# Graph attention with residual and layer norm on one core: normalising of finished rows moved from ScalarE to GpSimd, all but the last half chunk

## The reference

```python
mask = adj + eye > 0
Wh = (x @ W.T).reshape(n, 4, 32)
e = score_l[:, :, None] + score_r.T[None, :, :]      # per node and head
e = where(e >= 0, e, 0.2 * e)
e = where(mask[:, None, :], e, -inf)
alpha = softmax(e, axis=2)
out = elu(einsum('nhm,mhd->nhd', alpha, Wh).reshape(n, 128))
z = x + out
y = (z - mean(z)) / sqrt(var(z) + 1e-5)              # over the 128 features
```

## Time and profile before

| | us |
|---|---|
| median of 3 runs | 1782.24 |
| lowest and highest of the 3 | 1779.88, 1790.67 |
| the profiled execution, its own time | 1779.54 |
| its span, from the first to the last instruction | 1777.8 |

### The profile page before, as it was taken

One profiled execution on the slowest core, in us unless ns is written; L12 is line 12 of the kernel. 1 busy time (PEld: TensorE's weight loads), 2 busy tenths in 40 slices (PEclk: granted clock), 3 DMA queues, 4 the chain that ended last, 5 costly groups with the idle time before them and its releaser, 6 DMA issues. The chain is left out here.

```text
span 1777.8 us, 80971 instructions
## 1 busy us (share of the span) xinstructions
PE 1647.8 (93%) x37067; PEld 1626.5 (91%) x37067; DVE 1685.2 (95%) x1905; ACT 1667.8 (94%) x1246; POOL 26.2 (1%) x36
## 2 busy tenths in 40 slices
PE   6788898999999999999999999999999999999995
PEld 6788798899999999999999999999999998999995
DVE  6999999998979989999999999999899999999997
ACT  4999999989899999999999999999999999999992
POOL 0000000000001000000000100000000100000000
PEclk9899999999999999999999999999999999999998
DMA  8996888999998876675766676676667131121111
GB/s 278 344 346 206 277 293 266 341 313 328 310 307 293 257 246 198 205 243 182 244 202 223 207 242 215 209 235 208 224 189 236 35 82 58 37 58 37 35 37 37
DMA packets 241476, 368.10 MB, mean 207 GB/s; under 512 B 12912, under 2 KB 103408, under 8 KB 239600
## 3 DMA queue, kind: packets, MB, share of 16 engines
q1 hardware_dynamic: 241136, 362.92, 62.9%
HBM read 345.57 MB, written 17.30 MB: 204 GB/s over the span
## 5 line engine op out<-in xcount | busy, mean ns | idle before, releaser
L505 ACT ACTIVATE bmask<-lrow,rtab 128x2048 fp8e4<-128x2048 f32 (+1 forms) x975 | 1547.9, 1666 | 49.8 <-PE psum L414 47.5
L414 PE MATMUL psum<-vring,cmask 128*128 128x99 bf16 x14336 | 716.4, 208 | 30.5 <-DVE cmask L730 26.5
L414 PE MATMUL psum<-vring,bmask 128*128 128x99 bf16 x14336 | 722.0, 208 | 19.2 <-issue 15.6
L414 PEld LDWEIGHTS psum<-vring,cmask 128*128 128x128 fp8e4 x14336 | 662.0, 98 | 42.5 <-DVE cmask L730 35.8
L414 PEld LDWEIGHTS psum<-vring,bmask 128*128 128x128 fp8e4 x14336 | 667.4, 97 | 21.3 <-issue 17.5
L730 DVE SCALAR_TENSOR_TENSOR cmask<-acache,bmask 128x1024 int32<-128x1024 int32 x512 | 623.5, 1218 | 19.8 <-PE psum L414 19.5
L725 DVE SCALAR_TENSOR_TENSOR bmask<-acache,bmask 128x1024 int32<-128x1024 int32 x512 | 624.1, 1219 | 8.4 <-ACT bmask L505 4.6
L706 DVE TENSOR_SCALAR bmask<-lrow,rtab 128x2048 fp8e4<-128x2048 f32 (+1 forms) x305 | 316.8, 1052 | 0.0
L383 PE MATMUL trp<-pack,abuf 128*128 128x64 bf16 x4096 | 143.9, 194 | 32.3 <-ACT acache L474 23.5
L383 PEld LDWEIGHTS trp<-pack,abuf 128*128 128x128 bf16 x4096 | 132.6, 99 | 35.2 <-issue 35.0
L414 PE MATMUL psum<-vt,bmask 128*128 128x99 bf16 x2048 | 107.1, 211 | 12.2 <-issue 9.7
(11 more groups left out here) (64 smaller groups left out, 264.1 us busy)
## 6 DMA issues: line engine op xcount, KB each, us to landing
abuf<-in_adj_dram SPq DMA_DIRECT2D x256, 1024.0 KB, 8.4
vring<-v_scratch SPq DMA_DIRECT2D x384, 99.0 KB, 2.9
lrow<-l_scratch SPq DMA_DIRECT2D x16, 1024.0 KB, 7.9
v_scratch<-vt SPq DMA_DIRECT2D x16, 792.0 KB, 11.2
vring<-v_scratch SPq DMA_DIRECT2D x64, 198.0 KB, 6.0
cmask<-in_x_dram SPq DMA_DIRECT2D x16, 256.0 KB, 5.0
late<-in_x_dram SPq DMA_DIRECT2D x16, 256.0 KB, 5.2
out_dram<-late SPq DMA_DIRECT2D x16, 256.0 KB, 3.6
```

Source lines behind the costliest of these rows:

```text
L414: return nc.tensor.matmul(psum[:, bank, at * S3:(at + 1) * S3], mask[:, j * P:(j + 1) * P], values, start=opening, stop=True, skip_group_c ...
L505: last = nc.scalar.activation(to, rows, ACT.Relu, bias=rtab[:, 2 * s + i, H + h:H + h + 1], scale=BIG, saturate=False)
```

## The change

ScalarE no longer normalises entries 0 to 3 (8 + 8 + 16 + 16 = 48 groups) between its compares. GpSimd does so, in its loop over `FINISHED`, right after the power and a wait for `nmr_done`. Entry 4 stays with ScalarE at the end and entry 5 with VectorE. The semaphore that SP waits for, and its values, are the same.

```diff
@@ @block.scalar
-            def normalise(e, js):
-                act.wait_ge(nmr_done, e + 1)
-                for j in js:
-                    nc.scalar.activation(zz[:, j], zz[:, j], ACT.Identity, bias=nmr[:, j:j + 1], scale=vrs[:, j:j + 1]).then_inc(y_ready, 1)
-
@@
                 if s == 5 and w > 0:
                     elu_exp(w - 1)
-                for e, (done, js) in enumerate(FINISHED):
-                    if w == done + 1 and 13 <= s < 13 + len(js) // 2:
-                        normalise(e, js[2 * (s - 13):2 * (s - 13) + 2])
             elu_exp(PASSES - 1)
             elu_exp(PASSES)
-            normalise(len(FINISHED) - 2, FINISHED[-2][1])
+            e, js = len(FINISHED) - 2, FINISHED[-2][1]
+            act.wait_ge(nmr_done, e + 1)
+            for j in js:
+                nc.scalar.activation(zz[:, j], zz[:, j], ACT.Identity, bias=nmr[:, j:j + 1], scale=vrs[:, j:j + 1]).then_inc(y_ready, 1)
@@ @block.gpsimd
                 nc.gpsimd.tensor_tensor(mine, mine, epsc[:, JC:JC + len(js)], ALU.pow).then_inc(vrs_done, 1)
+                if e < len(FINISHED) - 2:
+                    pool.wait_ge(nmr_done, e + 1)
+                    for j in js:
+                        nc.gpsimd.tensor_scalar(zz[:, j], zz[:, j], vrs[:, j:j + 1], nmr[:, j:j + 1], ALU.mult, ALU.add).then_inc(y_ready, 1)
```

## The result

The change makes the kernel slower: 1802.62 us median of 4 runs (1799.04 to 1807.76) against 1784.86 of 4 runs of the kernel before beside it; ratio 1.0112, 95% interval [1.0091, 1.0134]. The forecast was 1783, with a range of 1775 to 1798.

What follows compares the result with a forecast made beforehand. Three engines were balanced, with VectorE bounding pass 12 and TensorE close in pass 8. Pass 12 -1.35 + 2.4 = +1.05, pass 8 -0.3, passes 2 and 4 0: +0.75 us, forecast 1783 on a 1782.24 median, range 1775 to 1798.

Steps and rivals of the forecast that it cites:

- The likeliest case: Whole kernel: small costs and gains cancel, about 1 us slower, 1783 us; chance 0.57, own range 1778 to 1789.
- GpSimd is starved and the stores are late: Rival, step 24 of passes 8 and 12: SP stands at the store, TensorE about 12 us each; +24, 1806; chance 0.08.
- What bounds the kernel, and ScalarE's relief: VectorE bounds pass 12, TensorE nearly pass 8; ScalarE is seldom waited for, so 2.15 of 18.7 us removed is gained.
- A group will take about one VectorE instruction plus itself, 1.5 us: GpSimd beside VectorE: 1.15 + 0.35 us a group, ends 0.3 and 3.4; 16 groups take 24 us.
- the add's 1.11 us: GpSimd's 128x16 add in pass 8, against 0.29 for 128x8 at the end: read as waiting for VectorE's instruction to end.
- The power's 4.58 us: GpSimd's power beside VectorE, against 1.64 for half its elements: taken to suggest that GpSimd can miss a turn.
- 36.1 us of room: Pass 12, from nmr ready at 1402.74 to the stores' start at 1438.85; 24 us needed, so the move costs nothing.
- 6 us of lateness are free: SP's stores: source-value loads run three steps ahead, so 6 us beyond 36.1 cost nothing; price begins at 2.6 us per group.
- the 1.19 us of the earlier trace: Pass 8: TensorE's other large wait, for a load, which the forecast said this change leaves.
- VectorE's loss, x = 0.15 us a group: VectorE's next instruction starts later: 2.4 us in pass 12; in pass 8 2.4 us meets 2.46 us of returned gaps.
- The rival of whole instructions held: Steps 13 on of passes 8 and 12: GpSimd holds VectorE, x = 0.6 us; +20, 1802; chance 0.15.
- The Trainium skill's rule of the exclusive lock: Shared SBUF port pair: VectorE or GpSimd locks it for a whole instruction, the loser blocks; x would be the whole instruction.

Runs made afterwards that it cites:

- e3: Changed kernel with its 48 GpSimd tensor_scalars replaced by one-column memsets, those rows left unnormalised: 1779.45 us, ratio 0.9994 to the kernel before.
- e7: Kernel before plus unawaited GpSimd work: memsets (passes 2, 4), 128x16 per-row tensor_scalars (pass 8), 128x128 constant ones (pass 12): 1780.93 us in one run.
- e1: Kernel before plus the 48 GpSimd tensor_scalars on a spare tile nobody waits for, and 8 at the start: 1783.47 us against 1782.06, ratio 1.0016.
- e5: Changed kernel with each entry's 8 or 16 GpSimd tensor_scalars replaced by two wide tensor_tensors: 1795.24 us, ratio 1.0070 to the kernel before.
- e9: e8 with three compares (steps 14, 20, 25) of passes 8 and 12 moved from VectorE to ScalarE: 1780.43 us against 1783.37, ratio 0.9980.
- e10: Kernel before with three compares (steps 14, 20, 25) of passes 8 and 12 moved from VectorE to ScalarE: 1792.47 us, ratio 1.0042.
- e8: Changed kernel with the stores of passes 4, 8, 12 and next x loads issued by GpSimd instead of SP: 1781.72 us, ratio 0.9992 to the kernel before.
- e6: Changed kernel with SP's stores moved from step 24 to 31 and x loads from 28 to next pass's step 2: 1782.02 us, ratio 0.9998 to the kernel before.

## Why the prediction was wrong

The likeliest case, 1783 us, failed; the rival "GpSimd is starved and the stores are late" (0.08, 1806) is what happened, at the place, by the links and from about the point that it named, and it gave 1806 where 1802.62 came. That its number is so near is in part luck. It took 3.4 us a group and 6 us of free lateness in each pass; with the 45.03 us that 16 groups took its own sum would be 45.03 - 42.1 = 2.9 us a pass. What made up for that is the lateness that was not free in pass 8, and the clock (points 2 and 3).

1. **What bounds the kernel, and ScalarE's relief.** Right in kind, high in size: 2.15 us of 18.7 forecast, 1.3 us in e3's passes, and no measurable change in its time. That ScalarE is full ahead of the others held.
2. **"A group will take about one VectorE instruction plus itself, 1.5 us."** This is the step that failed. It measured 2.90. The part "itself" was nearly right (0.45 alone, 0.35 taken). The number of VectorE instructions to be waited for was taken as one, by the add's 1.11 us, which reads two tensors and has no per-row operands. The power's 4.58 us I read as an exception, and my 1.64 beside it was for half its elements. The trace of before has the same 128x8 form in passes 2 and 4, of which the second took 3.2 us more than the 1.64 alone and the first 0.4 more:

```profile
340.76 2.08 POOL L958 TENSOR_TENSOR vrs<-vrs,epsc 128x8 f32<-128x8 f32 x1
...
569.51 4.83 POOL L958 TENSOR_TENSOR vrs<-vrs,epsc 128x8 f32<-128x8 f32 x1
```

e7 shows that extra turns come with the per-row operands: 1.29 us with constants, 2.7 to 2.9 with two of them. 16 groups took 45.03 us, not 24, against 36.1 us of room.

3. **"6 us of lateness are free", price from 2.6 us per group.** Half right. In pass 12 SP stood 10.5 us and TensorE waited 4.85, so 5.6 were free. In pass 8 SP stood 8.2 us and TensorE waited 8.74: nothing was free. There two block loads stand between the store and the source values, which land in 8.50 us, against 2.9 in pass 12. I had looked at the room in pass 12 only, where no blocks are loaded any more. And the kernel before showed it already: in its pass 8 the same load, issued at 1033.02 us behind the same two, took 9.0 us to land, and the 1.19 us of the earlier trace rows, at 1042.04, are TensorE's wait for just this load. I had read that wait as one that the change leaves alone; it says that no lateness is free there.

```profile
1031.24 1.74 SPq L229 DMA_DIRECT2D abuf<-in_adj_dram  x2
1033.02 7.26 SPq L260 DMA_DIRECT2D vring<-v_scratch  x4
```

The clock's fall after the stall (2.25 us in pass 8, 2.37 in pass 12) was not in the sum.

4. **VectorE's loss, x = 0.15 us a group.** It is 0.09 in the instruction that is stretched, and 0.07 to 0.08 by the sum: VectorE's busy time rose by 1.16 us in pass 8 and 1.34 in pass 12, for 16 groups each. The rival of whole instructions held (0.15, 1802) gave a time even nearer to the measured one, by luck, and is refuted by e1: all 48 instructions together cost 0.5 to 5 us.
5. **The Trainium skill's rule of the exclusive lock** (page "SBUF — State Buffer", on the shared port pair) deserved more weight than I gave it. I had set the 0.04 us beside the power against it. e5 shows VectorE standing 3.4 us beside one wide GpSimd instruction, as the rule says for whoever comes second. In two things the measurements differ from it, and they decide: beside a group of 128 elements VectorE lost 0.09 us and not the 0.45 that the group takes alone, and GpSimd waited over two, three and once twelve instructions of VectorE for one turn.

The chances were wrong rather than the list: the trace of before had two kinds of instruction on GpSimd beside VectorE, the add (0.8 us more than alone) and the power (0.4 to 3.2 us more in the same form), and the sum rested on the kinder one.

## What to carry to other kernels

Before work is moved to an idle engine, look for what waits in order behind its result: here not a computing engine but SP's list, where one late store held back every load after it. An in-order list can be without slack at one store and have some at the next: a wait for the load behind the store, as in the earlier trace rows, says that there is none. A short instruction on GpSimd beside a busy VectorE is to be priced by the VectorE instructions that it waits for, and not by its elements: here one with constants, mostly two or three with two per-row operands, and once twelve. Large instructions shorten the wait by making VectorE stand instead. And relief for an engine that is busy but not waited for brings nothing until its freed time is given other work (e3 against e9 and e10).

## What was new about the hardware

- A tensor_scalar of 128x128 on GpSimd with two per-row operands takes 0.45 us alone and 2.9 in the mean beside VectorE's two-input instructions (0.45 to 14.9 for single ones); with constants 1.29; a memset 0.205 in both places.
- VectorE lost 0.09 us per such GpSimd instruction, and 3.4 us per tensor_tensor of 128x2048.
- Stores and loads issued by GpSimd itself (e8) did their work beside a busy VectorE at 0.8 and 0.7 us per issue, with no loss in the kernel's time. Its stores landed 7.7 us after their issue in the median, those of SP in the kernel before 3.6; why is open.
- After 8.74 us without work TensorE ran at a granted clock of 0.51 for its next 64 products (5.45 us instead of 3.2), after 4.85 us at 0.50 as well, and in e5 a wait of 2.40 us was followed by the lower level too. After most waits of 1 to 2 us it stayed at the higher level: 32 products after a wait of 1.19 us took 1.61 us. But not after all: in e6, in pass 3, the granted clock was 0.50 soon after a wait of 1.92 us.

```profile
501.61 1.14 PE L416 MATMUL psum<-vring,bmask 128*128 128x99 bf16 x19 [1.92 <-issue]
502.54 2.87 PE L416 MATMUL psum<-vring,cmask 128*128 128x99 bf16 x32
```
